# A GRU and block attention on one core: four blocks' attention made inside the last steps, sigmoids in place of exponentials, an unsplit last step

## What is computed

```python
def cell(h, x):
    gi = x @ W_ih + b_ih
    gh = h @ W_hh + b_hh
    r = sigmoid(i_r + h_r)
    z = sigmoid(i_z + h_z)
    n = tanh(i_n + r * h_n)
    return (1.0 - z) * n + z * h
x1 = x + scan(cell, cond, x)                   # 64 steps in a row
block_repr = x1.reshape(B, 8, 8, 512).sum(axis=2)
keys = einsum('bnh,kh->bnk', block_repr, Wk)
keys = keys / sqrt(mean(keys * keys) + EPS) * rms_weight
attn = softmax(einsum('bnh,h->bn', keys, q))   # q = cond[1]
proj = einsum('bn,bnh->bh', attn, block_repr) @ Wo.T
y = x1 + proj                                  # proj is the same for all 64 tokens of b
out = x1 + (y - mean(y)) / sqrt(var(y) + EPS) * ln_gamma + ln_beta
```

## Time and profile before

| | us |
|---|---|
| median of 3 runs | 375.47 |
| lowest, highest | 374.59, 376.02 |
| the profiled execution, its own time | 376.31 |
| its span, first to last instruction | 374.2 |
| TensorE busy / VectorE / ScalarE / GpSimd | 362.1 / 264.3 / 158.6 / 15.3 |
| mean granted TensorE clock | 0.995 |

### The profile page before, as it was taken

One profiled execution on the slowest core, in us unless ns is written; L12 is line 12 of the kernel. 1 busy time (PEld: TensorE's weight loads), 2 busy tenths in 40 slices (PEclk: granted clock), 3 DMA queues, 4 the chain that ended last, 5 costly groups with the idle time before them and its releaser, 6 DMA issues.

```text
span 374.2 us, 9793 instructions
## 1 busy us (share of the span) xinstructions
PE 362.1 (97%) x3267; PEld 212.2 (57%) x3267; DVE 264.3 (71%) x1138; ACT 158.6 (42%) x506; POOL 15.3 (4%) x47
## 2 busy tenths in 40 slices
PE   8899999999999999999999999999999999997895
PEld 5355555666665556666555666655566666334672
DVE  2746667777676778686768767676778676768897
ACT  3501326262534344352626262534344364756510
POOL 5013000000000000000000000000000000100000
PEclk9999999999999999999999999999999999998999
DMA  7985544323232322324141323232322322110038
GB/s 269 403 322 159 165 102 151 103 68 102 72 98 70 93 68 56 98 59 109 44 106 40 98 70 98 70 98 70 78 75 65 97 56 72 49 45 16 17 138 312
DMA packets 28100, 40.05 MB, mean 107 GB/s; under 512 B 3120, under 2 KB 19120, under 8 KB 28080
## 3 DMA queue, kind: packets, MB, share of 16 engines
q1 hardware_dynamic: 28080, 39.79, 36.5%
HBM read 19.60 MB, written 4.19 MB: 64 GB/s over the span
## 4 chain that ended last, share of the span: by engine, by line
PE 86%; DMA 5%; DVE 4%; SPq 1%; ACT 1%; issue 1%; DVEq 0%
PE gates_ps L601 43%; PE gi_ps L570 36%; DMA gcx<-in_w_ih_dram 3%; DMA w_hh<-in_w_hh_dram 2%; PE third_ps L601 1%; PE keys_ps L601 1%; PE fourth_ps L601 1%; PE keys_ps L711 1%; SPq L268 1%; PE first_ps L730 1%; DMA h_tok<-hist 1%; SPq L259 1%; PE keys_ps L678 1%; PE gi_ps L671 1%; PE gi_ps L583 1%
## 5 line engine op out<-in xcount | busy, mean ns | idle before, releaser
L601 PE MATMUL gates_ps<-w_hh,turned 128*32 128x384 f32 x1920 | 167.3, 489 | 0.5 <-DVE turned L805 0.5
L601 PEld LDWEIGHTS gates_ps<-w_hh,turned 128*32 128x32 f32 x1920 | 56.5, 109 | 85.5 <-issue 56.4
L570 PE MATMUL gi_ps<-w_ih_hi,xt_hi 128*128 128x384 f32 x240 | 86.8, 364 | 0.0
L570 PE MATMUL gi_ps<-w_ih_hi,xt_lo 128*128 128x384 f32 x240 | 80.7, 338 | 0.0
L570 PE MATMUL gi_ps<-w_ih_lo,xt_hi 128*128 128x384 f32 x240 | 79.7, 334 | 0.0
L460 ACT ACTIVATE rz<-gates_ps 128x256 f32<-128x256 f32 x60 | 23.1, 385 | 128.7 <-PE gates_ps L601 128.6
L869 DVE TENSOR_TENSOR rz<-gates_ps,rz 128x128 f32<-128x128 f32 x60 | 17.5, 291 | 79.4 <-ACT rz L460 79.4
L570 PEld LDWEIGHTS gi_ps<-w_ih_hi,xt_hi 128*128 128x128 f32 x240 | 44.9, 187 | 37.5 <-issue 36.8
L570 PEld LDWEIGHTS gi_ps<-w_ih_lo,xt_hi 128*128 128x128 f32 x240 | 45.1, 188 | 0.0
L570 PEld LDWEIGHTS gi_ps<-w_ih_hi,xt_lo 128*128 128x128 f32 x240 | 44.9, 187 | 0.0
L805 DVE STREAM_TRANSPOSE turned<-hist 128x32 f32<-128x32 f32 (+1 forms) x192 | 36.7, 216 | 2.2
(11 more groups left out here) (209 smaller groups left out, 294.6 us busy)
## 6 DMA issues: line engine op xcount, KB each, us to landing
gi<-gi_tok SPq DMA_DIRECT2D x60, 192.0 KB, 3.4
x1t<-in_x_t_dram SPq DMA_DIRECT2D x16, 256.0 KB, 3.2
gcx<-in_x_tok_dram SPq DMA_DIRECT2D x16, 256.0 KB, 3.2
h_tok<-hist SPq DMA_DIRECT2D x64, 64.0 KB, 2.2
out_dram<-gcx SPq DMA_DIRECT2D x16, 256.0 KB, 2.3
gcx<-in_w_ih_dram SPq DMA_DIRECT2D x4, 768.0 KB, 8.5
w_hh<-in_w_hh_dram SPq DMA_DIRECT2D x4, 768.0 KB, 9.0
wo_t<-in_wo_t_dram SPq DMA_DIRECT2D x1, 1024.0 KB, 5.7
```

Source lines behind the costliest of these rows:

```text
L570: mm = pe.matmul(gi_ps[tok][:, 0:G3], a[:, k, :], w[:, k, gi_cols(j)], start=(m == 0), stop=(m == 3 * NJ - 1))
L601: mm = pe.matmul(gates_bank(t)[j * B:(j + 1) * B, P:], before[:, k * B:(k + 1) * B], chunk(w_hh, k, j), start=False, stop=(k == NJ - 1), s ...
```

## The change

Four parts, all in the last block and behind it.

1. Attention over blocks 0 to 3 is made inside the last steps. The group's keys are read a step earlier (`keys_dot(0)` in step 4), `key_rms` is made in two halves on GpSimd, `early_scores` gives the four scores, a matmul into `keys_ps[:, 0:4]` lays them out, and `early_attention` on VectorE at the end of step 5 makes `att_early`. `att_first` then starts from it and adds blocks 4 to 6. With it, the reduce into `last_part` goes from step 4 to step 2, `split_s2` to step 3, `lay_s2` to step 6, and the sum over steps 4 to 6 of the block becomes three adds.
2. The softmax uses sigmoids: a weight against a reference score is s / (1 - s) with s = sigmoid(difference), and the last block's share is itself a sigmoid, `last_weight`, of scale `last_rms` and bias `neg_max`. Both exponentials, the larger maximum and the differences go; a reciprocal and a product come. The denominator is made behind `cp`'s turn.
3. The last step works on whole 128 x 128 tiles (`last_step`), one instruction where there were two or three.
4. The last quad's `add_turned` stands behind the instruction that releases GpSimd's power; in the output stage the cross product of the last four quads goes ahead of `lay_x1(4)`. `keep_warm_again` adds three matmuls without a reader: one behind the last step's gates, two behind `lay_x1(1)`.

The diff, cut to its core and indented less:

```diff
+    for group in range(2):
+        pool.wait_ge(key_var_ready, group + 1)
+        pool.tensor_tensor(key_rms[:, group:group + 1], key_ss[:, group:group + 1], half[:, 0:1], ALU.pow
+                           ).then_inc(key_rms_ready, 1)
     pool.wait_ge(last_var_ready, 1)
     pool.tensor_tensor(last_rms, last_var, half[:, 0:1], ALU.pow).then_inc(last_rms_ready, 1)
...
+        if last and s == S - 1:
...
+            act.activation(rz[:], gates_ps[:, P:3 * P], ACT.Sigmoid).then_inc(rz_ready, 1)
+            act.wait_ge(n_pre_ready[0], T)
+            act.activation(n[:], n[:], ACT.Tanh).then_inc(n_ready, 1)
+            return
         wait(act, gates_ready, t + 1)
         act.activation(rz[:], gates_bank(t)[:, P:3 * P], ACT.Sigmoid).then_inc(rz_ready, 1)
-        seeds = not (last and s == S - 1) and not (isinstance(t, int) and t < Q - 1)
...
             add_beta(NQ - 2)
+            act.wait_ge(early_max_ready, 1)
+            act.activation(early_odds, keys_ps[:, 0:4], ACT.Sigmoid, bias=early_neg_max[:, 0:1]
+                           ).then_inc(early_odds_ready, 1)
             add_beta(NQ - 1)
...
     act.wait_ge(max_ready, 1)
-    act.activation(probs, fourth_ps[:, 0:NB - 1], ACT.Exp, bias=neg_max[:, 0:1],
-                   accum_out=prob_sum).then_inc(probs_ready, 1)
+    act.activation(odds[:, 0:1], early_neg_max[:], ACT.Sigmoid, bias=neg_max, scale=-1.0)
+    act.activation(odds[:, 1:4], fourth_ps[:, 4:7], ACT.Sigmoid, bias=neg_max).then_inc(odds_ready, 1)
...
-    act.wait_ge(top_step, 4)
-    act.activation(share, top, ACT.Exp).then_inc(share_ready, 1)
-    act.wait_ge(share_ready, 1)
-    act.activation(denom, prob_sum, ACT.Identity, scale=share[:, 0:1], bias=share[:, 1:2]
-                   ).then_inc(denom_step, 1)
+    act.wait_ge(last_rms_ready, 1)
+    act.activation(last_weight, fourth_ps[:, 1:2], ACT.Sigmoid, bias=neg_max, scale=last_rms
+                   ).then_inc(last_weight_ready, 1)
+    act.wait_ge(last_weight_ready, 1)
+    act.wait_ge(last_proj_ready, 1)
+    act.activation(cp, gates_ps[:, 0:P], ACT.Copy, scale=last_weight).then_inc(cp_step, 1)
     act.activation(scalar_warm[:], half[:, 0:1], ACT.Sqrt, scale=-1.0).then_inc(warmed, 1)
...
         if last and s == 5:
+            pe.wait_ge(early_score_ready, 1)
+            pe.matmul(keys_ps[:, 0:4], same_b[:], early_n, start=True, stop=True).then_inc(early_ps_ready, 1)
+        if last and s == 6:
             pe.wait_ge(s2_split, 1)
             pe.wait_ge(mask_ready, 1)
             lay_s2(0, NQ - Q, small_ps, P)
...
+    def keep_warm_again(times):
+        for _ in range(times):
+            pe.matmul(keys_ps[:], xt_hi[:, 0, :], w_ih_hi[:, 0, 0:D], start=True, stop=True)
+    pe.wait_ge(early_odds_ready, 1)
+    keep_warm_again(1)
     pe.wait_ge(score_ready, 1)
     pe.matmul(fourth_ps[:, 0:NB], same_b[:], score_n[:].rearrange("p h n -> p (h n)"),
               start=True, stop=True).then_inc(scores_ps_ready, 1)
...
     pe.wait_ge(beta_added, NQ)
     lay_x1(0)
     lay_x1(1)
+    keep_warm_again(2)
...
     pe.wait_ge(last_dot_ready, 1)
...
-    pe.wait_ge(probs_ready, 1)
+    pe.wait_ge(odds_ready, 1)
     pe.matmul(fourth_ps[:, 0:2], same_b[:], last_key, start=True, stop=True).then_inc(last_sums_ready, 1)
     lay_x1(2)
...
-    for _ in range(2):
-        pe.matmul(keys_ps[:], xt_hi[:, 0, :], w_ih_hi[:, 0, 0:D], start=True, stop=True)
+    keep_warm_again(2)
...
     lay_s2(NQ - Q, Q, fourth_ps, 4 * Q)
-    lay_x1(4)
     pe.wait_ge(x1t_ready, NQ)
     cross_sums(2, 3)
+    lay_x1(4)
     lay_x1(5)
...
+        if last and s == 2:
+            dve.tensor_reduce(last_part, x1t[:, NQ - 1].rearrange("p k (b t) -> p (k b) t", t=Q), AX.X,
+                              ALU.add).then_inc(pre_step, 1)
+        if last and s == 4:
+            keys_dot(0)
+            key_var(0)
+        if last and s == 5:
+            dve.wait_ge(early_ps_ready, 1)
+            dve.tensor_reduce(early_neg_max[:], keys_ps[:, 0:4], AX.X, ALU.max, negate=True
+                              ).then_inc(early_max_ready, 1)
...
+        if last and s == 3:
+            split_s2(0, NQ - Q)
         if last and s == 4:
-            dve.tensor_reduce(last_part, x1t[:, NQ - 1].rearrange("p k (b t) -> p (k b) t", t=Q), AX.X,
-                              ALU.add).then_inc(pre_step, 1)
-            split_s2(0, NQ - Q)
-        if last and s == 5:
-            keys_dot(0)
             dve.wait_ge(pre_step, 1)
             dve.wait_ge(part_ready, NQ - 1)
             dve.tensor_tensor(last_part, last_part, parts_t[:, 0, :], ALU.add).then_inc(pre_step, 1)
+            add_to_part(s, 2)
+            early_scores()
+        if last and s == 5:
+            early_attention()
         if last and s == 6:
-            dve.wait_ge(ht_ready, 3 * T)
-            dve.tensor_reduce(last_hs, turned[:, Q:S - 1, :].rearrange("p t c -> p c t"), AX.X, ALU.add
-                              ).then_inc(pre_step, 1)
             keys_dot(1)
-            dve.wait_ge(key_sq_ready, 2)
-            dve.tensor_scalar(key_ss[:], key_ss[:], 1.0 / D, EPS, ALU.mult, ALU.add
-                              ).then_inc(key_var_ready, 1)
-            dve.wait_ge(pre_step, 3)
-            dve.tensor_tensor(last_part, last_part, last_hs, ALU.add).then_inc(pre_step, 1)
+            key_var(1)
+            add_to_part(5, 3)
+            add_to_part(6, 4)
...
+    def key_var(group):
...
+        dve.wait_ge(key_sq_ready, group + 1)
+        dve.tensor_scalar(key_ss[:, group:group + 1], key_ss[:, group:group + 1], 1.0 / D, EPS, ALU.mult, ALU.add
+                          ).then_inc(key_var_ready, 1)
+    def add_to_part(s, number):
+        dve.wait_ge(pre_step, number)
+        dve.wait_ge(ht_ready, ((NB - 1) * S + s) * 3 + 6)
+        dve.tensor_tensor(last_part, last_part, turned[:, s, :], ALU.add).then_inc(pre_step, 1)
+    def early_scores():
+        dve.wait_ge(key_rms_ready, 1)
+        dve.wait_ge(key_dot_ready, 1)
+        dve.tensor_tensor(score[:, 0:1], key_dot[:, 0:1], key_rms[:, 0:1], ALU.mult).then_inc(early_step, 1)
+        dve.wait_ge(early_step, 1)
+        dve.tensor_scalar(early_n, own_n[:], score[:, 0:1], None, ALU.mult).then_inc(early_score_ready, 1)
...
+    def early_attention():
+        dve.wait_ge(early_odds_ready, 1)
+        dve.tensor_scalar(early_rest, early_odds, -1.0, 1.0, ALU.mult, ALU.add).then_inc(early_step, 1)
+        dve.wait_ge(early_step, 2)
+        dve.reciprocal(early_rest, early_rest).then_inc(early_step, 1)
+        dve.wait_ge(early_step, 3)
+        dve.tensor_tensor_reduce(early_weights, early_odds, early_rest, 1.0, 0.0, ALU.mult, ALU.add,
+                                 sums_of[:, 0:1]).then_inc(early_weights_ready, 1)
+        dve.wait_ge(early_weights_ready, 1)
+        dve.tensor_scalar(att_early, br_all[:, 0:P], early_weights[:, 0:1], None, ALU.mult).then_inc(early_step, 1)
+        for nb in range(1, 4):
+            dve.wait_ge(early_step, 3 + nb)
+            dve.scalar_tensor_tensor(out=att_early, in0=br_all[:, nb * P:(nb + 1) * P],
+                                     scalar=early_weights[:, nb:nb + 1], in1=att_early,
+                                     op0=ALU.mult, op1=ALU.add).then_inc(early_step, 1)
...
+    def last_step():
+        centre_tokens(NQ - 2)
+        score_keys()
+        dve.wait_ge(rz_ready, T)
+        dve.tensor_tensor(r, gates_ps[:, 3 * P:], r, ALU.mult).then_inc(rh_ready, 1)
+        dve.wait_ge(rh_ready, T)
+        dve.tensor_tensor(n[:], r, gi[:, 1, (Q - 1) * G3:(Q - 1) * G3 + P], ALU.add).then_inc(n_pre_ready[0], 1)
+        dve.tensor_tensor(zh[:], z, hist[:, S - 2, :], ALU.mult).then_inc(terms_ready, 1)
+        dve.wait_ge(scores_ps_ready, 1)
+        dve.tensor_reduce(neg_max, fourth_ps[:, 0:NB - 1], AX.X, ALU.max, negate=True
+                          ).then_inc(max_ready, 1)
+        dve.wait_ge(n_ready, 2 * T - 1)
+        dve.scalar_tensor_tensor(out=n[:], in0=z, scalar=1.0, in1=n[:], op0=ALU.subtract, op1=ALU.mult
+                                 ).then_inc(terms_ready, 1)
+        dve.wait_ge(terms_ready, 5 * T - 3)
+        dve.tensor_tensor(hist[:, S - 1, :], zh[:], n[:], ALU.subtract).then_inc(h_ready, 1)
+        dve.wait_ge(h_ready, 3 * T - 2)
+        dve.transpose(turned[:, S - 1, :], hist[:, S - 1, :]).then_inc(ht_ready, 1)
...
+    for s in range(S - 1):
         step(NB - 1, s, last=True)
-    dve.wait_ge(ht_ready, 3 * T + 3)
-    dve.wait_ge(pre_step, 4)
+    last_step()
+    dve.wait_ge(ht_ready, 3 * T + 1)
+    dve.wait_ge(pre_step, 5)
     dve.wait_ge(br_saved, NB - 1)
     dve.tensor_tensor(br_turned[:], last_part, turned[:, S - 1, :], ALU.add).then_inc(turned_ready, 1)
-    dve.tensor_scalar(top[:, 0:1], neg_max, -1.0, None, ALU.mult).then_inc(top_step, 1)
...
+    dve.wait_ge(odds_ready, 1)
+    dve.tensor_scalar(rest_of, odds, -1.0, 1.0, ALU.mult, ALU.add).then_inc(weights_ready, 1)
+    dve.wait_ge(weights_ready, 1)
```

(46 more changed lines are left out.)

69 lines of the change are left out of this document (33 added, 36 removed).

## The result

| | before | after |
|---|---|---|
| median of 20 runs each | 375.16 | 374.50 |
| lowest, highest | 373.97, 377.31 | 373.80, 375.20 |
| the profiled execution, its own time | 376.31 | 373.8 |
| its span | 374.2 | 371.8 |
| TensorE / VectorE / ScalarE / GpSimd busy | 362.1 / 264.3 / 158.6 / 15.3 | 361.5 / 266.2 / 157.6 / 16.6 |

The ratio after to before is 0.9975, 95% interval 0.9963 to 0.9986: a gain of 0.9 us, 0.5 to 1.4, which is real and lies within half a per cent. The two profiled executions differ by 2.5, more than the medians do: that of before is among its longer ones, that of after its shortest.

A forecast was written before the change was run, and what follows sets the result against it. TensorE and the state's links bound the kernel up to step 63, and TensorE the output stage. Terms 0.68 + 1.34 + 0.76 - 0.80 - 0.50 = 1.48, mixed to 1.04 off 375.47, gave 374.4, range 373.1 to 375.8.

The forecast's parts named there:

- last step on whole tiles: Step 63, r product to `br_turned`: one row of whole-tile instructions takes 1.90 instead of 2.58, gain 0.68.
- clock, in an execution with the fall: TensorE's two `br_turned` products: warm matmuls keep the clock up, 3.45 becomes 2.10, gain 1.34.
- mean square to `cp`, without the lock: Last key's mean square to the add making `cp`: 1.66 instead of 2.42 if the power is not held, gain 0.76.
- the add beside the power: Behind the last mean square: VectorE's two-input add starts first and blocks GpSimd's power, cost 0.80, bounds 0 and 0.9.
- denominator: Behind `cp`'s turn: three small VectorE instructions now stand ahead of add_tokens, cost 0.50.
- What this move buys elsewhere I cost at nothing.: Output stage: taking the last quad's add out of it gains 0, its chain being TensorE's.
- The sign that I named as one of being wrong: Output stage, profile after: VectorE's idle time staying what it was would show the prediction wrong.
- The mix: Kernel before: some two in three executions have the clock fall; gain 0.14 without it, 1.48 with it, mixed 1.04.
- D: Rival, attention's part before `cp`: early attention is worth nothing under the forecast; its chance lies within the forecast's 0.50.
- B: Rival, last step: the clock falls all the same, time 376.1, or 375.7 from the mix; chance 0.14.
- Rival A: Behind the last mean square: GpSimd's power runs beside the add unblocked, time 373.6; chance 0.28.
- C: Slower rival, behind 346: the clock falls and stays low twice as long, TensorE waiting between shorter pieces, 377.1; chance 0.05.

The follow-up runs named there:

- f1_power_first: Changed kernel with the denominator ahead of `cp`'s add, and the attention's turn and weights' sum ahead of the last quad's add: median 372.89 us, six runs.
- e2_one_input: Changed kernel with the last quad's add back in the output stage and two unread one-input VectorE reductions beside the power: median 373.79 us.
- f2_no_early_back: Changed kernel without the early attention and with the last quad's add back in the output stage: median 375.12 us.
- e1_add_back: Changed kernel with the last quad's add and the pair of cross product and layout back as before in the output stage: median 373.83 us.
- e6_best: Changed kernel with the last quad's add back in the output stage and the denominator made ahead of `cp`'s add: median 374.12 us.
- b1_add_beside: Kernel before with only the last quad's add moved behind the instruction that releases the last key's power: median 376.68 us.
- a_again: The changed kernel run once more, unaltered, as yardstick for the other runs: median 374.25 us, ratio 0.9977 to the kernel before.

## Why the prediction was right

Forecast 374.4, measured 374.50, inside the range, and within half a per cent as the likeliest case had it. The mechanism was the predicted one, the lock with a full clock. That the number meets to 0.1 is in part luck: the gain was forecast as 1.04 and is 0.9 by the ratio, 0.66 by the medians, and it was counted from the median of three executions, 375.47, where twenty gave 375.16. The terms:

| term | forecast | measured | from |
|---|---|---|---|
| last step on whole tiles | 0.68 | 0.59 | 2.58 to 1.99 |
| clock, in an execution with the fall | 1.34 | 1.40 to 1.43 | 4.15 to 2.75 or 2.72 |
| mean square to `cp`, without the lock | 0.76 | 0.75 | 2.42 to 1.67 |
| the add beside the power | -0.80 | -0.80 | 2.47 against 1.67 |
| denominator | -0.50 | -0.59 | 4.84 to 5.43 |
| output stage without the add | 0 | 0.30 | 18.71 to 18.41 |
| sum | 1.48 | 1.68 | the changed kernel behind the r product |

- *Last step.* Right but for 0.09: the starts follow each other at 0.32 to 0.34, a little wider than durations and handovers of other lines gave.
- *The add beside the power.* Right by the same account: the power waits for the add's end and then takes 0.4. The hundredth is luck, for the working gave 0.73 to 0.92. The rule from SBUF — State Buffer, section Who interferes with whom, of the Trainium skill, is borne out in the direction that the earlier trace rows could not show, for two SBUF inputs (1.34) against one (0.55). What the section says of VectorE's two-port modes, that whoever issues first has the shared pair for the whole instruction, does not carry over to `f1_power_first`: the power was first, and the add was not held.
- *"What this move buys elsewhere I cost at nothing."* This step failed, and so did the nothing for the exchange beside it. I argued that the output stage's chain is TensorE's. But the one handover of 0.04 in that chain is TensorE waiting for the add (x1t) before the second cross product, which then takes 1.08 where it takes 1.01 behind other matmuls; and the stage does not end with the chain's last matmul but with the stores. In four pairs that differ by the add and the exchange the stage was shorter without the add by 0.25 to 0.51 (`e2_one_input`, `f2_no_early_back`, `e1_add_back`, `e6_best`, against 18.41, 18.45, 18.41 and 18.40), 0.15 of it on TensorE and the rest in the stores. The sign that I named as one of being wrong did not come: VectorE's idle time in the stage rose, from 3.24 to 3.76.
- *The mix.* "Some two in three" of the old kernel's executions with the fall was read from three times and a profile. It was 28 in 99. So the fall's cure brought about 0.28 x 1.43 = 0.40 to the mean and not 0.9 (two thirds of 1.34), while the gain without the fall was 31.47 - 31.02 = 0.45 and not 0.14. The two errors cancelled: 0.85 in the sum against my 1.04.
- *The early attention* fits in step 5 as worked out, with nothing to spare (its last pass ends at 335.86 and the r product starts at 335.90), and steps 5 to 6 take 4.89, against 4.88 before. *D*, that it is worth nothing under the lock, was wrong by 0.3: without it the projection, and not the power, ends last, and `cp` comes 0.33 later.
- *Small slips.* The addends from the mean square to `cp` make 1.67 and not 1.66; B's two times come to 376.2 and 375.8, not 376.1 and 375.7. None moves the forecast.
- *The table load* behaves as the earlier trace rows had it: the square root's begins at 347.85, takes 1.28, and the next instruction starts at 349.14.
- *Rival A* fell with the power's 1.34. *B* fell: no fall of that size in 32 executions. *C* did not come in the changed kernel, but its mechanism is real: it is what made `b1_add_beside` slow.
- *Start of the program.* 0.72 of the profiled pair's difference is no part of the change. Against one profile I would have called the sum 2.40.

## What to carry to other kernels

In these runs a short GpSimd operation on a critical path waited for whichever VectorE instruction with two SBUF inputs was running when it arrived, and only for that one. So put long ones behind its start, by some 0.15 us (0.13 here) of one-input or small work, rather than right behind its release: 1.34 became 0.55 with the same work in the same wait. Before costing a move out of a stage at nothing, look for handovers in the chain, however small, that wait for what moves, and for what ends the stage behind the chain's last matmul. And where a slow execution comes in some runs only, count them over many before giving it a weight.

## What the runs showed of the hardware that was not expected

- The lock is taken per instruction, as far as these runs tell: beside three 0.35 passes with two SBUF inputs the power lost 0.04 (0.59 against 0.55), beside one of 1.09 it lost 0.79. The passes themselves were not slowed (1.12 for three, with or without the power beside them).
- The power in front does not hold VectorE: the add begun 0.13 behind it took 1.09. Near 30 us a 128x512 product of GpSimd held a VectorE product for over 1 us, so the size of GpSimd's operand may be what counts; that was not tested.
- One kernel, with the same lists, had a mean clock of 0.995 or less in 28 of 99 executions and 0.996 or more in the others, 1.43 apart in the mean; in the one profiled with it the fall lay at the end of the last step. A profiled execution shows one of the two and not how often it comes.
- A fall at the very end costs nothing: in `a_again` the clock was 0.58 from 370.00 to 372.80, when TensorE had no matmul left, and its output stage was 18.47 against 18.41. A mean clock of 0.997 alone therefore does not tell that time was lost; where the fall lies does.
